# A 2.8-ms graph and expert program: zeroing, node weights and pair additions redistributed, expert lookup with wider copies, and the first attention layer's normalization, value order and masks rearranged

## The reference

```python
y = (x - mean) * rsqrt(var + EPS) * (1.0 + cond @ sw + sb) + (cond @ bw + bb)
q, k, v = y @ wq + bq, y @ wk + bk, y @ wv + bv
scores = einsum('ehd,ehd->eh', q[src], k[dst])
out = segment_sum(softmax_over_edges_of(src, scores) * v[dst], src)
x = x + out @ wo + bo
x = x + relu(norm2(x) @ m_w1 + m_b1) @ m_w2 + m_b2
```

## Time and profile before

| | us |
|---|---|
| median of three runs | 2829.57 |
| the profiled execution | 2829.51 |
| its span, first to last instruction | 2827.8 |
| input projection | 51.05 |
| edges | 454.4 |
| node update, norm, routing | 40.7, 40.3, 40.2 |
| experts | 280.8 |
| first rows stage | 129.7 |
| everything behind it | 1785.4 |

### The profile page before, as it was taken

One profiled execution on the slowest core, in us unless ns is written; L12 is line 12 of the kernel. 1 busy time (PEld: TensorE's weight loads), 2 busy tenths in 40 slices (PEclk: granted clock), 3 DMA queues, 4 the chain that ended last, 5 costly groups with the idle time before them and its releaser, 6 DMA issues. The chain is left out here.

```text
span 2827.8 us, 38792 instructions
## 1 busy us (share of the span) xinstructions
PE 2473.0 (87%) x13385; PEld 2137.4 (76%) x13385; DVE 1800.0 (64%) x3380; ACT 1446.1 (51%) x3097; POOL 1181.6 (42%) x870
## 2 busy tenths in 40 slices
PE   4899999439674879999989989989999999998999
PEld 3778777338474768877978877978878778777997
DVE  2888888544733646777457776367676367677852
ACT  2677767413345646655346654356654266545431
POOL 2688888753764533243012251022260032363420
PEclk9999999659687899999999999999999999999999
DMA  6754454149355841011111021121022120221101
GB/s 178 207 114 98 106 108 88 12 127 287 76 161 150 231 141 36 19 56 55 52 55 37 19 58 64 41 64 44 1 73 70 51 59 19 66 64 34 57 15 34
DMA packets 177931, 228.02 MB, mean 81 GB/s; under 512 B 113804, under 2 KB 126279, under 8 KB 170318
## 3 DMA queue, kind: packets, MB, share of 16 engines
q1 hardware_dynamic: 90987, 197.04, 23.7%
q0 software_dynamic: 86752, 28.51, 6.0%
HBM read 177.10 MB, written 40.15 MB: 77 GB/s over the span
## 5 line engine op out<-in xcount | busy, mean ns | idle before, releaser
L2264 POOL TENSOR_SCALAR prob<-prob,rden,linked 125x1250 f32<-125x1250 f32 x160 | 224.0, 1400 | 840.9 <-DVE rden L2231 840.9
L649 POOL DMA_INDIRECT pairs<-late_cnt,late_idx x160 | 344.8, 2155 | 125.0 <-DMA pairs<-late_cnt,late_idx 75.0
L2182 ACT CAST prob_high<-ps 125x375 fp32r<-125x375 f32 (+1 forms) x480 | 231.4, 504 | 266.3 <-PE ps L2144 266.0
L2223 DVE CUSTOM_DVE_ANT_0 prob<-ps,mask 125x1250 f32<-125x1250 f32 x160 | 233.1, 1457 | 129.4 <-PE ps L2120 110.0
L2236 DVE TENSOR_TENSOR prob_low<-ps,prob_high 125x375 fp32r<-125x375 f32 (+1 forms) x480 | 269.7, 585 | 46.6 <-ACT prob_high L2182 46.6
L2133 PE MATMUL ps<-ident,prob 125*125 125x125 f32 x1600 | 252.3, 273 | 17.2 <-POOL prob L2264 10.6
L608 PE MATMUL ps<-onehot,mhi 125*128 125x512 f32 (+1 forms) x960 | 246.2, 365 | 21.2 <-DVE onehot L483 19.8
L374 POOL DMA_INDIRECT Hg<-h_rows,dsti x160 | 219.2, 1370 | 94.1 <-issue 64.7
L2133 PEld LDWEIGHTS ps<-ident,prob 125*125 125x125 f32 x1600 | 232.3, 187 | 29.7 <-POOL prob L2264 22.9
L608 PE MATMUL ps<-onehot,mlo 125*128 125x512 f32 (+1 forms) x960 | 239.2, 358 | 0.0
L2174 ACT ACTIVATE prob<-prob,top 125x1250 f32<-125x1250 f32 x160 | 214.7, 1342 | 45.9 <-DVE top L2223 37.0
(11 more groups left out here) (453 smaller groups left out, 5947.2 us busy)
## 6 DMA issues: line engine op xcount, KB each, us to landing
mask<-mask_d SPq DMA_DIRECT2D x40, 546.9 KB
sg_wd<-L_ffn_Wd SPq DMA_DIRECT2D x32, 512.0 KB, 7.1
w_ring<-L_ffn_Wd SPq DMA_DIRECT2D x16, 1024.0 KB, 14.7
w_ring<-L_ffn_Wu SPq DMA_DIRECT2D x16, 1024.0 KB, 5.4
pairs<-zeros POOLq DMA_DIRECT2D x18, 625.0 KB
keyrow<-keys_d SPq DMA_DIRECT2D x40, 244.1 KB
kept<-g_d SPq DMA_DIRECT2D x40, 224.0 KB
g_d<-kept SPq DMA_DIRECT2D x30, 224.0 KB
```

Source lines behind the costliest of these rows:

```text
L649: nc.gpsimd.indirect_dma_start(pairs[a][:, :], bass.IndirectOffsetOnAxis(T.E.late_idx[:, c:c + 1], 0), T.E.late_cnt[:, c:c + 1], None, com ...
L2182: s.copy(M.pt[0][:, n % 3, 0:w], T.ps[0:P, 3 + n % 4, 0:w]).then_inc(high, 1)
L2223: v.tensor_tensor_reduce(M.prob[:, r, :], S(u)[0:P, 0:N], M.mask[:, it % MASKS, :], 1.0, 3.0e38, ALU.add, ALU.min, M.top[:, r:r + 1]).then ...
L2264: nc.gpsimd.tensor_scalar(M.prob[:, r, :], M.prob[:, r, :], M.rden[:, r:r + 1], T.linked[:, it:it + 1], ALU.mult, ALU.mult).then_inc(norme ...
```

## The change

- Zeroing of array 0: four of the eleven parts stay in the input projection, each behind a number of finished copies; seven go to the edges, behind fetch(0) and fetch(1).
- Edges: 62 additions instead of 60, the paced ones 58 instead of 54; the node weights are loaded by SP at group 20; ScalarE's copy and fill of the stack go behind softplus(0), VectorE's subtraction behind act_sum(0). Node update: no loads, TensorE waits on `nu_in`. Shares: 62, 14, 10, 74.
- Experts: wq is loaded before the stores of y. `chunk` puts the low halves in banks 0 and 1 and the high halves in 2 to 5, with a wait each; `look` makes two predicated copies of 1024 columns a tile instead of four of 512.
- First rows stage: the rows that come in have been normalized once already; their mean is taken as 0 and their variance as var · rstd² from the stage before, so one square root for all tiles (`deviations`) and one reciprocal (`all_scales`) take the place of statistics and scales per tile. V goes over the tiles in the order 5, 6, 3, 4, 2, 1, 0, 7, 8, 9; logarithm and cap of tiles 8 and 9 go into its loop; POOL's masks and counts are in a new order; SP does `late` before store_mask(4); the wait for the next conditions goes to SP's end; four pair buffers have new addresses; `linked` is made after V.
- All layers: each load of 17 condition rows is made as 16 + 1, and the bias loads of 125 rows (bv, m_b2, bo) as 112 + 13.

```diff
-EARLY_ADDS = 60
-PACED_ADDS = 54
+EARLY_ADDS = 62
+PACED_ADDS = 58
...
-                    for part in range(ZEROS):
+                    for part in range(ZEROED_FIRST):
+                        pool.wait_ge(copied, 2 * part + 1)
                         zero_pairs(nc, T, pairs, 0, part)
...
+                        if g == NG // 2:
...
+                            sp.dma_start(w2v[:], A["L0_gnn_w_f2o2_v"]).then_inc(T.nu_in, 16)
...
                     fetch(0)
                     fetch(1)
+                    for part in range(ZEROED_FIRST, ZEROS):
+                        zero_pairs(nc, T, pairs, 0, part)
...
+                    s.mul(minus[:], srcf[:], -1.0).then_inc(far, 1)
+                    features(0)
+                    bend(0)
+                    softplus(0)
                     s.copy(w_stack[0:3 * FF, :], E.w2[0:3 * FF, :, :].rearrange("p k f -> p (k f)")).then_inc(w_stacked, 1)
...
-LATE = (EARLY_ADDS, EARLY_ADDS + 16, EARLY_ADDS + 28, ET)
+LATE = (EARLY_ADDS, EARLY_ADDS + 14, EARLY_ADDS + 24, ET)
...
+                    sp.dma_start(place.raw_b[:].rearrange("p k n -> p (k n)"),
+                                 A["L1_gnn_wq"][0:1].rearrange("a c d -> (a c) d")).then_inc(rows_in, 16)
                     for t in range(NS_T):
                         sp.wait_ge(yc_act, t + 1)
...
-                        if q >= 3:
-                            pe.wait_ge(low, q - 2)
-                            pe.wait_ge(high, q - 2)
                         for u in range(2):
                             g = 4 * c + 8 * u
-                            ins = mm(T.ps[:, 2 * (q % 3) + u, :], R.hot[:, t * 128:(t + 1) * 128],
+                            if u == 0 and q >= 2:
+                                pe.wait_ge(low, q - 1)
+                            if u == 1 and q >= 4:
+                                pe.wait_ge(high, (q - 4) // 2 + 1)
+                            ins = mm(T.ps[:, (q % 2, 2 + q % 4)[u], :], R.hot[:, t * 128:(t + 1) * 128],
...
+                        for a in range(2):
+                            dve.wait_ge(low, 4 * t + 2 * a + 2)
+                            v.copy_predicated(sel[:, u, a, 0:8, :], mask(0, t).broadcast_to([128, 8, HID]),
+                                              T.ps[:, 2 + 2 * a:4 + 2 * a, :].rearrange("p b (g h) -> p (b g) h", g=4)).then_inc(high, 1)
...
-LOG_AT = (2, 4, 6, 9, 11, 13, 15, 17, 19, 22)
-CAP_AT = (3, 5, 8, 10, 12, 14, 16, 18, 20, 23)
+LOG_AT = (2, 4, 6, 9, 11, 13, 16, 21)
+CAP_AT = (3, 5, 8, 10, 12, 14, 17, 22)
+LOG_V = {1: 8, 3: 9}
+V_ORDER = (5, 6, 3, 4, 2, 1, 0, 7, 8, 9)
...
+                late(sp, cw_ready, cw_next, made, a_in, unit_made, v_in)
+                if masks:
                     store_mask(4)
                     sp.wait_ge(mask_out[3], 32)
                     load_pairs(8)
-                late(sp, cw_ready, cw_next, made, a_in, unit_made, v_in)
-                if masks:
                     store_mask(5)
...
                     mask(5)
+                    mask(6)
+                    mask(7)
                     count(8)
-                    mask(6)
                     count(9)
-                    for t in range(7, NT):
-                        mask(t)
+                    mask(8)
+                    mask(9)
...
+                def deviations():
+                    act.wait_ge(step, 2)
+                    s.activation(T.std[:], T.std[:], ACT.Sqrt, bias=T.eps[0:P, :]).then_inc(std_s, 1)
...
+                    for i, t in enumerate(v_order):
+                        act.wait_ge(v_row, i + 1)
+                        if masks and t == 5:
+                            act.wait_ge(mask_made, 8)
...
+                        if masks and i in LOG_V:
+                            logarithm(LOG_V[i])
+                            cap(LOG_V[i])
...
+                def all_scales():
+                    v.tensor_tensor(T.std[:], T.mv[:, :, 1], T.rstd[:], ALU.mult).then_inc(step, 1)
+                    v.memset(T.shift[:], 0.0).then_inc(scale_s, 1)
+                    dve.wait_ge(step, 1)
+                    v.tensor_tensor(T.std[:], T.std[:], T.rstd[:], ALU.mult).then_inc(step, 1)
+                    dve.wait_ge(std_s, 1)
+                    v.reciprocal(T.rstd[:], T.std[:]).then_inc(scale_s, 1)
...
+                            if masks and t == 3:
+                                dve.wait_ge(mask_made, 9)
+                            if masks and t == 2:
+                                dve.wait_ge(mask_made, NT)
...
-                sp.dma_start(T.cw[r:r + CH + 1, :, :].rearrange("p j d -> p (j d)"), one(par(f"cond{k}", L))).then_inc(cw_in, 16)
+                rows, src = T.cw[r:r + CH + 1, :, :].rearrange("p j d -> p (j d)"), one(par(f"cond{k}", L))
+                sp.dma_start(rows[0:CH, :], src[0:CH, :]).then_inc(cw_in, 16)
+                sp.dma_start(rows[CH:CH + 1, :], src[CH:CH + 1, :]).then_inc(cw_in, 16)
...
-                sp.dma_start(bvo[:, 0, :], bro("bv", L)).then_inc(v_in, 16)
+                wide(sp, bvo[:, 0, :], bro("bv", L), v_in)
                 sp.dma_start(flat(M.raw_b), one(par("wv", L))).then_inc(v_in, 16)
-                sp.wait_ge(cw_next, 48)
```

More of the change, by code:

```diff
@@ L1605, in rows_stage @@
         masks = pairs is not None
+        v_order = V_ORDER if masks else range(NT)
         if masks:
@@ L1674, in _ @@
                     sp.wait_ge(stored, 32 * NT)
+                if three or not last:
+                    sp.wait_ge(cw_next, 96)
             @block.gpsimd
@@ L1836, in center @@
                 def center(t):
-                    act.wait_ge(scale_s, 2 * t + 2)
+                    act.wait_ge(scale_s, 2 if source == "first" else 2 * t + 2)
                     if t >= 4:
@@ L1883, in masking @@
                 def masking(n):
-                    for t in range(NT) if masks else ():
+                    for t in range(len(LOG_AT)) if masks else ():
                         if n == LOG_AT[t]:
@@ L1893, in _ @@
                     o_hi(1)
+                if source == "first":
+                    deviations()
                 s.copy(M.cwr[:], T.cw[:]).then_inc(cw_ready, 1)
@@ L2001, in _ @@
                     split(M.raw_a, M.a, a_high, a_cut)
+                if source == "first":
+                    all_scales()
                 dve.wait_ge(cw_ready, 1)
@@ L2033, in _ @@
                             split(M.raw_a, M.a, k_high, k_cut)
+                if three:
+                    for i in range(NT + 1):
+                        if i < NT:
+                            dve.wait_ge(v_made, i + 1)
+                            if i >= 4:
+                                dve.wait_ge(v_low, i - 3)
+                            v.tensor_tensor(M.y[:, i % 4, :], T.ps[0:P, i % 4, :], bvo[:, 0, :], ALU.add).then_inc(v_row, 1)
+                        if i >= 1:
+                            t = v_order[i - 1]
+                            dve.wait_ge(v_top, i)
+                            if masks and t == 5:
+                                dve.wait_ge(mask_out[5], 32)
+                            if masks and t == 3:
+                                dve.wait_ge(mask_made, 9)
+                            if masks and t == 2:
+                                dve.wait_ge(mask_made, NT)
+                            if masks and t == 7:
+                                dve.wait_ge(mask_out[9], 32)
+                            v.tensor_tensor(M.v[1][:, t, :], M.y[:, (i - 1) % 4, :], M.v[0][:, t, :].bitcast(F32),
+                                            ALU.subtract).then_inc(v_low, 1)
                 if masks:
@@ L2322, in rest @@
                 sp.dma_start(flat(M.raw_a), one(par("wo", L))).then_inc(rest_in, 16)
[L2323 to L2324 removed]
+                wide(sp, bvo[:, 1, :], bro("bo", L), rest_in)
+            attention(nc, T, M, mask_d, rest, 48)
             rows_stage(nc, T, M, "attn", "mlp", g_d, x_d, *mlp_loads(L, last), bvo[:, 1, :], bqk, bvo, last=last)
```

102 lines of the change are left out of this document (34 added, 68 removed).

## The result

The changed kernel takes 2798.83 us (median of 4 runs, 2794.91 to 2799.82), the kernel before 2827.97 in the same comparison: a ratio of 0.990, 95% interval 0.9882 to 0.9917. It is 29 us faster, not 45. The profiled execution took 2799.82 us (span 2798.1), 29.7 less than the one of before.

| stage | before | after | difference | forecast |
|---|---|---|---|---|
| input projection | 50.7 | 42.3 | −8.4 | −8.2 |
| edges | 454.5 | 471.5 | **+17.0** | −2.7 |
| node update | 40.7 | 35.8 | −4.9 | −4.5 |
| norm | 40.2 | 35.8 | −4.5 | −4.5 |
| routing | 40.3 | 39.9 | −0.4 | 0 |

A forecast was written before the change was run, and what follows sets the result against it. Ahead of TensorE's dense layers, eight barrier-ended stages cost whatever ends last. Terms −8.2 (input), −2.7 (edges), −4.5 (node update), −4.5 (norm), −8.9 (experts), −16.7 (first rows) sum to −45.5: 2829.5 to 2784 us, range 2774 to 2799.

The forecast's parts named there:

- I take +1, with bounds 0 and +5: Edge stage: seven zeroing parts moved beside the stack and key loads cost 1 us, at most 5.
- R1: Rival, edge stage: moved zeroing collides with gathers and stack load, costing +5 to +12; about 2795 us, chance 0.15.
- The −3.1 of the start: Edge stage start: ScalarE's features(0) no longer stands behind copy and fill, saving 3.1 us of 3.9.
- 88 left: Edge loop: POOL has 349 of 437 us filled and 88 left, so four more paced additions stay hidden.
- 0, at most +2: Experts: two more additions end at 875.3, before y is stored, so they cost 0, at most 2 us.
- wq's −2.0: Experts: loading wq earlier keeps it off the DMA engines during the first gathers, saving 2.0 us.
- The 7.1 us for wv: First rows stage: TensorE's wait for the value weights goes through split condition loads and a new queue order, 7.1 us.
- The 3.5 ahead of the units: First rows stage: dropping per-tile statistics saves 3.5 us of TensorE's wait on y_row before the first q/k unit.
- The 4.7 inside the units: First rows stage: dropping per-tile statistics saves 4.7 us of TensorE's wait on y_row inside the q/k units.
- R2: Rival, first rows stage: V waits for masks instead of wv, so it gives 8 to 10 us; 2792 us, chance 0.16.
- R3: Rival, experts' look phase: VectorE shuts POOL out about 60 us, so the gather is late; 2844 us, chance 0.02.
- R4: Rival: ends of input, node update and norm have another cause than POOL's transfers, giving 8 of 17.2; 2793 us, chance 0.11.

The follow-up runs named there:

- experiment 1: Changed kernel with all eleven zeroing parts of array 0 back in the input stage: 2786.63 us, ratio 0.9862; edges 453.0 us.
- experiment 3: Changed kernel with four pair additions moved from the experts to the edges: 2798.25 us, ratio 0.9904; experts 271.8, edges 478.4 us.
- experiment 7: Changed kernel with the old lookup (four predicated copies of 512 columns a tile): 2801.43 us, ratio 0.9907; experts 280.1 us.
- experiment 12: The kernel of experiment 3 with wq loaded behind the stores of y again: 2803.18 us, ratio 0.9907; experts 273.1 us.
- experiment 4: Kernel before with only the split loads (conditions 16 + 1, biases 112 + 13): 2812.29 us, ratio 0.9952; first rows stage 122.5 us.
- experiment 8: Changed kernel with statistics, deviation, reciprocal and shift per tile back in the first rows stage: 2800.98 us, ratio 0.9912; that stage 115.1 us.
- experiment 10: Changed kernel with all ten logarithms and caps back in ScalarE's loop over the q/k units: 2814.1 us, ratio 0.9954; first rows stage 124.1 us.
- experiment 6: Changed kernel with six of the experts' pair additions made in routing: 2805.95 us, ratio 0.9929; routing 48.1, experts 273.7 us.
- experiment 9: Changed kernel with eight zeroing parts in input, the rest over five edge groups, and group 1's key rows first: 2792.3 us, ratio 0.9875.

## Why the prediction was off

*Input stage*: right, −8.4 for −8.2, by the mechanism given.

*Edge stage*: wrong, and this is where most of the difference lies. The step that failed is "I take +1, with bounds 0 and +5". The rival R1 named the mechanism and its place and was given +5 to +12 and 0.15; it came with a stall of some 19 us. The step's bound came from dividing a transfer time: 13.3 us of zeroing, of which a third might fall on the stack loads. Two things were not in it. First, a load that VectorE waits for was never named: the second group's key rows, issued behind twelve stack loads, which themselves slow down, so the delays add up in SP's queue. Second, the seven parts are not the last: two and three more follow with groups 0 and 1, 6.9 MB in all, which is 21 us at the 330 GB/s I used (of the seven the last two are smaller, 478.5 and 0.5 KB, so they were 3.7 MB and not 4.4). Had I walked SP's queue through the first three groups with these 21 us beside it, 19 us would have been in the bounds. The −3.1 of the start came as −2.4 to the first scatter, and without the burst (experiment 1) the stage is 1.4 us shorter than before, for −3.7 without the +1. The "88 left" on POOL were some 6 us where it mattered (experiment 3).

*Node update and norm*: −4.9 and −4.5 for −4.5 each. Right; the same norm code took 33.8 to 35.8 us in the other profiles.

*Experts*: −1.6 for −8.9. The term "0, at most +2" for two more additions is the one that failed. The last addition moved from 238.8 to 248.5 us into the stage, 9.7 us for two additions: their own time grew by 4.5 us, and their waits for each other's landing from 73.3 to 80.3 (some 3 us of it scatter, experiment 7). The lookup gained more than said: y's first store comes 9.0 us sooner, 7.1 by experiment 7, for the 6.9 of the pauses; the prediction took the copies at the same cost, and they are cheaper too. (It speaks of eight banks; the kernel uses six.) wq's −2.0 is not borne out (experiment 12). The lookup's gain ends in front of the additions (experiments 3, 7). I compared POOL's new end with y's old end, though the same change moved y's end forward by 9 us; the new one stood in my own sum.

*First rows stage*: −18.6 for −16.7, but the parts were put down to other causes, and that the sum lies near is in part luck. The 7.1 us for wv and the 1.4 of the clock are the split loads (experiment 4: −7.2 in all). The 3.5 ahead of the units are 3.8 (experiment 8). The 4.7 inside the units is the term that failed: the statistics cost 0.3 there. In its place the new order of the masks' work on ScalarE and POOL made the units shorter, 60.3 us instead of the 69.2 of experiment 4; experiment 10 shows that late logarithms can hold them, and not how the 8.9 divide. R2, the masks in wv's place, didn't come: V starts 79.6 us into the stage and TensorE waits for no mask (VectorE does, for 2.8 us).

*Layers*: 0 forecast, −8.4 between the two profiles. The eleven other kernels that hold the changed layers gave 1774.2 to 1782.6 in their profiles, and the kernel before with the split loads 1779.0, against its 1785.4. So some us may be the split loads of every layer, and some are what executions differ by; with one profile of the kernel before, how much is which stays open.

*R3*, POOL starved in the look phase: didn't come. Additions there took 1.97 to 3.12 us, before up to 2.83. With the rule of the Trainium skill, "SBUF — State Buffer", Practical consequences, by which predicated copies from PSUM shut nobody out, this agrees; what blocked the 9.64-us addition of the earlier trace rows was not tried.

*R4*: wrong in each of its three stages, which gave 17.8 us together.

*R1* named 2795, and 2798.83 was measured. That is near for a part by luck: the edge stage lost 17.0 us, not 5 to 12, and the 7.3 us missing in the experts and the 8.4 gained in the layers nearly cancel.

## What to carry to other kernels

A bulk transfer of no urgency that is moved out of one stage's end into the next stage's start must be checked against the first load that anyone waits for there, in the order of each queue, and together with the bulk that stands there already. Two or three parts of up to 625 KB in each group of edges held up no key rows by more than 1.9 us here; four, five or seven made stalls of 8.5 to 19 us. When two chains meet at a join, compare their new ends, not one's new with the other's old: a gain on one chain is worth no more than the distance to the next. And an engine's idle share over a long stretch is no room for more work: POOL looked a fifth idle and was full, by 0.30 us behind every transfer it issued. Ask whether the predecessor will have landed, where the work would go.

## What the runs showed that was not expected

An indirect addition that takes 2.0 us to issue can wait 10.15 us for the one two before it to land when 1-MB loads run beside it (experiment 6), and 15.3 us at most in the experts. The zeroing parts raised the issue of a small stack load from 0.6 to 1.9 us and made the 512-KB weight load behind the second group's key rows take 10.23 us of SP's queue, where it took 0.70 before. Loads of 17 rows made as 16 + 1, and the bias as 112 + 13, were worth 7.2 us by themselves (experiment 4).

The 116.9 us of the first rows stage in experiment 9, with the code that took 110.9 to 112.2 elsewhere, have a visible place. VectorE makes the low part of wk, there and then in the changed kernel:

```profile
945.21 10.48 DVE L1974 TENSOR_TENSOR set_a_low<-set_a_raw,set_a_high 128x512 fp32r<-128x512 f32 x4 [4.77 <-ACT set_a_high L1836]
954.73 2.55 DVE L1969 TENSOR_TENSOR set_a_low<-set_a_raw,set_a_high 128x512 fp32r<-128x512 f32 x4 [4.76 <-ACT set_a_high L1831]
```

Three of the four took up to 3.38 us instead of 0.68, and TensorE waited 4.0 us for them. POOL was in its mask operations on two inputs, of 2.9 to 3.4 us each, for nearly all of that time (945.09 to 955.13), and idle from 954.93 to 958.04 in the changed kernel. That the one slowed the other is likely from this and was not tested. A few us of shift between two engines can thus cost a stage 5 us.
